# Sorted experts of a two-layer network: gate and up weights become the stationary operand, copied ahead by ScalarE

## The chip, the cores and the metric

The kernel runs on one core of a Trainium2 chip. The metric is the time of one execution on the device, in microseconds, as the median of several executions. TensorE (PE in the rows) does matrix products and transposes, from SBUF into PSUM; VectorE (DVE), ScalarE (ACT) and GpSimd (POOL) do the rest; SyncE's queue (SPq) issues most of the DMAs.

## What is computed

The reference is a network of two layers over 8192 tokens of 128 features. Each layer multiplies an attention branch by a gated expert branch and adds the result to its input. The change lies in the last step, the routed experts of the second layer, where every token goes to one of 32 experts:

```python
topk_ids = jnp.argmax(x @ gate_w, axis=-1)
topk_val = jnp.max(x @ gate_w, axis=-1)
xs = x * jax.nn.sigmoid(topk_val)[:, None]
order = jnp.argsort(topk_ids)
sorted_x = xs[order]
g = _grouped_mm(sorted_x, routed_gate_w, tokens_per_expert)      # 128 -> 256, weights of the row's expert
u = _grouped_mm(sorted_x, routed_up_w, tokens_per_expert)        # 128 -> 256
d = _grouped_mm(jax.nn.silu(g) * u, routed_down_w, tokens_per_expert)  # 256 -> 128
routed_out = d[inv]
...
x = x + s * silu(shared_out + routed_out)
```

Everything is 32-bit float.

## The kernel before

The kernel has four stages, one after the other, with a barrier between them. The first two do the first layer, the third does the second layer's attention branch and the routing. It writes each token as one row of a DRAM tensor `srt`, at a slot that the routing gives it: 96 tiles (`SORTED_TILES`) of 128 rows, each tile with rows of one expert only. A row holds the scaled token (128 values), and behind it a tail of 400 values: a key that names the token, the residual, the attention branch and the shared expert's result. The third stage also leaves a small table `TE` in SBUF that names the expert of each tile; row j of it has eight numbers, those of the four tiles of chunk j-1 and those of the four of chunk j.

The fourth stage, `stage4`, works through the 96 tiles in 24 chunks of four (`IN_FLIGHT`, `n_t`). Chunks 0 and 1 and the last two are written out, those between run in a loop with two chunks in its body, for the two buffers b = 0 and 1. The weights of all 32 experts lie in SBUF (`WE1`, rows call it `big`): per expert 512 columns of gate and up, then 256 of down. For one tile:

- SyncE loads the scaled rows of a chunk (`load`, 256 KB) two chunks ahead, once TensorE has turned the rows that lay in the buffer, and the tails (`load_tail`, 800 KB), once the chunk two before is finished.
- TensorE turns the tile of rows (`row_transpose`, L2041), ScalarE copies it out of PSUM (`rows`, L2100) to `xT`.
- TensorE multiplies (`up`, L2036): the turned rows are the stationary operand, the expert's 512 gate and up columns move past it. The product has tokens in the partitions and hidden features along the row.
- ScalarE applies silu to the gate half (L2110), VectorE multiplies it by the up half (`product`, L2132) into `hb`.
- TensorE turns the product, in two pieces of 128 (`hidden_transpose`, L2046), and VectorE copies it back (`turned`, L2136) to `hT`.
- TensorE multiplies `hT`, stationary, by the down weights in two steps (`down`, L2055) into a quarter of PSUM bank `yp`.

TensorE's order of work is written out by hand. Around tile t it does up(t), the row transpose of t+2, the hidden transpose of t-2 and down(t-3). At the head of a chunk `experts` reads the eight numbers of a row of `TE` into registers (`TENSOR_LOAD`), and these give the addresses of the weights in `WE1`.

Per chunk VectorE adds the shared experts' part (`summed`, L2142), ScalarE takes the silu (`result`, L2104), VectorE multiplies and adds (`weigh` L2147, `finish` L2154 and L2155; the latter increments `done`), and GpSimd scatters the four tiles to the output by four indirect DMAs (`store`, L2191 and L2194). `finish` of chunk 21 stands in chunk 23 behind the product of its third tile, which is tile 94.

## Time and profile before

| | us |
|---|---|
| median of 3 executions | 1386.27 |
| lowest and highest | 1384.61 and 1388.18 |
| the profiled execution's own time | 1387.99 |
| its span, first to last instruction | 1385.5 |
| fourth stage: first row transpose starts | at 1185.99 |
| fourth stage: last store is issued | at 1376.39 |

The profile was taken from one execution, whose own time is 1.7 us above the median; 2.5 us of it lie outside the span. Times in the rows count from the start of the span. An f32 product appears as two records on TensorE, each with a weight load of its own (PEld), so that a product's records come in pairs; a transpose is one record. The idle time of an engine before a row stands in brackets, with what released it.

### The profile page before, as it was taken

Reading aid. Unit: us, or ns where it says so; the run is one execution under the profiler, and the core shown is the slowest. Engines: PE = TensorE matmul, PEld = TensorE weight load, DVE = VectorE, ACT = ScalarE, POOL = GpSimd, SP = SyncE. Lnnn points to the kernel's source line nnn. Section 1 sums busy time; section 2 is a strip of 40 time slices with the busy share of each in tenths; the row PEclk is TensorE's granted clock in tenths of the full one; section 3 lists DMA queues with packets and bytes.
Section 4 is the critical chain, followed back from the end, with each engine's and each line's share of the span. In section 5 each row is a group of like instructions: output and inputs, shape, how many; then the busy total and the mean of one; then the engine's idle time right before and its main releaser. Section 6 shows DMA issues by size and latency. Waiting matters only on the chain. (4 is left out here: it accounts for less than half of the span.)

```text
span 1385.5 us, 28473 instructions
## 1 busy us (share of the span) xinstructions
PE 1191.1 (86%) x7942; PEld 902.7 (65%) x7943; DVE 989.9 (71%) x3562; ACT 783.7 (57%) x1993; POOL 645.9 (47%) x1096
## 2 busy tenths in 40 slices
PE   5999999999972899999999956988888896799993
PEld 3778777777851677767677744766676674456662
DVE  3777777777777777777777636888888886366663
ACT  2575656666630666656565625777777774233331
POOL 3343434343312354545454523556555645056665
PEclk9999999999985999999999977999999999899997
DMA  4424242424301222222222113344344232356651
GB/s 163 144 96 143 88 154 85 150 92 144 127 24 38 51 50 59 44 61 42 61 42 61 35 37 94 113 140 133 120 138 144 91 134 89 119 163 189 184 175 52
DMA packets 140717, 140.83 MB, mean 102 GB/s; under 512 B 18662, under 2 KB 119885, under 8 KB 140672
## 3 DMA queue, kind: packets, MB, share of 16 engines
q1 hardware_dynamic: 125248, 111.38, 25.8%
q0 software_dynamic: 14848, 26.77, 6.9%
q10 hardware_dynamic: 576, 2.15, 0.4%
q8 instruction: 19, 0.31, 0.1%
q14 instruction: 26, 0.21, 0.0%
HBM read 67.63 MB, written 62.13 MB: 94 GB/s over the span
## 5 line engine op out<-in xcount | busy, mean ns | idle before, releaser
L377 ACT ACTIVATE pr<-ps,nmx 128x256 f32<-128x256 f32 x256 | 117.9, 474 | 43.9 <-DVE nmx L424 42.8
L365 ACT ACTIVATE big<-ps,BHS 128x256 f32<-128x256 f32 x256 | 107.1, 470 | 61.3 <-PE ps L242 52.5
L242 PE MATMUL ps<-big,W 128*128 128x256 f32 x512 | 130.9, 400 | 5.6 <-ACT big L370 5.5
L255 PE MATMUL ps<-W,big 128*128 128x128 f32 x1024 | 130.7, 281 | 0.0
L255 PEld LDWEIGHTS ps<-W,big 128*128 128x128 f32 x1024 | 119.6, 192 | 14.0 <-ACT big L365 6.0
L2194 POOL DMA_INDIRECT out<-X,io x96 | 100.5, 1047 | 34.4 <-issue 34.4
L242 PEld LDWEIGHTS ps<-big,W 128*128 128x128 f32 x512 | 95.7, 197 | 26.9 <-ACT big L370 15.7
L2036 PE MATMUL ps<-big,zT 128*128 x192 | 102.5, 616 | 9.6 <-DVE pr L2132 9.1
L424 DVE TENSOR_REDUCE nmx<-ps 128x2 f32<-128x512 f32 x128 | 82.4, 686 | 38.5 <-PE ps L277 21.4
L1003 POOL DMA_INDIRECT ffn<-big,si x64 | 94.0, 1468 | 26.5 <-issue 26.5
L2110 ACT ACTIVATE pr<-ps 128x256 f32<-128x256 f32 x96 | 36.9, 384 | 108.5 <-PE ps L2036 95.4
L432 DVE COPY pT<-ps 128x512 f32<-128x512 f32 x128 | 82.6, 686 | 9.8 <-PE ps L286 9.1
L2132 DVE TENSOR_TENSOR pr<-ps,pr 128x256 f32<-128x256 f32 x96 | 40.7, 424 | 65.7 <-ACT pr L2110 63.3
L510 POOL TENSOR_TENSOR big<-big,EPS 128x2 f32<-128x2 f32 x32 | 6.7, 210 | 155.0 <-DVE big L459 155.0
L277 PE MATMUL ps<-qk 64*128 64x256 f32 x512 | 73.5, 406 | 2.6 <-DVE v L417 2.6
L295 PE MATMUL ps<-pT,v 128*64 128x256 f32 x512 | 69.4, 392 | 3.8 <-DVE pT L432 0.5
L262 PE MATMUL ps<-zT,W 128*128 128x256 f32 x256 | 72.6, 408 | 0.0
L286 PE MATMUL ps<-CST,pr 128*128 128x128 f32 x512 | 68.4, 276 | 1.0 <-ACT pr L377 1.0
L286 PEld LDWEIGHTS ps<-CST,pr 128*128 128x128 f32 x512 | 56.5, 141 | 15.9 <-issue 7.7
L370 ACT ACTIVATE big<-ps,COL 128x256 f32<-128x256 f32 x64 | 36.1, 564 | 53.8 <-PE ps L232 53.8
L415 DVE SCALAR_TENSOR_TENSOR qk<-ps,COL,ROT 128x256 f32<-128x256 f32 x128 | 55.0, 471 | 11.9 <-PE ps L266 9.8
L450 DVE SCALAR_TENSOR_TENSOR big<-ps,rsm,X 128x128 f32<-128x128 f32 x128 | 39.0, 347 | 34.1 <-PE ps L304 25.2
(280 smaller groups left out, 3233.9 us busy)
## 6 DMA issues: line engine op xcount, KB each, us to landing
srt<-big SPq DMA_DIRECT2D x16, 1584.0 KB, 5.7
X<-srt SPq DMA_DIRECT2D x24, 800.0 KB
big<-we SPq DMA_DIRECT2D x16, 768.0 KB, 7.6
big<-we SPq DMA_DIRECT2D x16, 384.0 KB, 3.5
X<-srt SPq DMA_DIRECT2D x24, 256.0 KB
big<-x SPq DMA_DIRECT2D x32, 128.0 KB, 2.2
X<-big SPq DMA_DIRECT2D x32, 128.0 KB, 2.2
xw<-big SPq DMA_DIRECT2D x32, 128.0 KB, 1.9
```

Source lines behind the costliest of these rows:

```text
L242: last = pe.matmul(pb[2 * g + f // 2][:, f % 2 * S:(f % 2 + 1) * S], W0[:, l, 512 + f * P:512 + (f + 1) * P], zT2[:, g, :], start=True, st ...
L255: last = pe.matmul(pb[4 + g][:, t * C:(t + 1) * C], hT[:, g, f, t * P:(t + 1) * P], W0[:, l, 1024 + f * C:1024 + (f + 1) * C], start=(f == ...
L262: pe.matmul(pb[4 + g][:, j * S:(j + 1) * S], w, zT1[:, g, :], start=True, stop=True)
L277: last = pe.matmul(pb[2 * g + h][:, t * S:(t + 1) * S], qk[d, g, 0, t * P:(t + 1) * P], qk[d, g, 1, :], start=True, stop=True)
L286: last = pe.transpose(pb[2 * g + h][:, k * S + t * P:k * S + (t + 1) * P], pr[:, g, h, t, k * P:(k + 1) * P], ident)
L365: act.activation(hT[:, g, f, :], pb[2 * g + half][:, f % 2 * S:(f % 2 + 1) * S], ACT.Silu, bias=BHS[:, l, f:f + 1], scale=GELU).then_inc(s ...
L377: last = act.activation(pr[:, g, h, t, :], pb[2 * g + h][:, t * S:(t + 1) * S], ACT.Exp, bias=nmx[:, g, h * TPU + t:h * TPU + t + 1], accu ...
L424: last = dve.tensor_reduce(nmx[:, g, h * TPU:(h + 1) * TPU], pb[2 * g + h].rearrange("p (t k) -> p t k", t=TPU), X_AXIS, ALU.max, negate=True)
L432: dve.tensor_copy(pT[:, g, h, :, :].rearrange("p k q -> p (k q)"), pb[2 * g + h])\
L1003: pool.indirect_dma_start(out=ffn0[:, :], out_offset=bass.IndirectOffsetOnAxis(ap=si[:, n:n + 1], axis=0), in_=ye[half, n // 2, :], in_off ...
L2036: pe.matmul(gu(k), xT[k % n_t], WE1[:, e, 0:2 * F1], start=True, stop=True).then_inc(s["gu"], 1)
L2194: pool.indirect_dma_start(out=out[:, :], out_offset=bass.IndirectOffsetOnAxis(ap=io[b][:, k:k + 1], axis=0), in_=ob[b][:, k, :], in_offset ...
```

## The change

The gate and up product changes sides. ScalarE copies the 512 gate and up columns of a tile's expert out of `WE1` into one of four fixed buffers `wu` (freed tensors of earlier stages: z, v, att and ROT), four tiles ahead of the silu that stands before the copy. TensorE then uses the four blocks of 128 columns as stationary operands, with the turned rows moving past them, in four products of 128 columns where there was one of 512. The product comes out with hidden features in the partitions, as `down` wants its stationary operand, so that the two hidden transposes of a tile and the copy `turned` are gone. `gu` gets four PSUM banks instead of two. The copy of the turned rows moves from ScalarE to VectorE.

TensorE's order around tile t becomes up(t+2), row transpose of t+4, down(t). The read of a row of `TE` moves on TensorE from the head of a chunk to behind the chunk's first up, and ScalarE reads a row per chunk too. VectorE's `finish` moves from behind the third product of a chunk to behind the first, so that `finish` of chunk 21 stands behind tile 92; `summed` moves from the end of a chunk to behind the second product of the same chunk, `weigh` from the second product to the fourth, of the chunk before. The table `TE` is made by fewer instructions.

```diff
@@ -1842,18 +1842,15 @@
                     def table_rows():
+                        n_c = SORTED_TILES // IN_FLIGHT
+                        dve.memset(TE[:, 0:1, 0:IN_FLIGHT], 0)
+                        dve.memset(TE[:, n_c:n_c + 1, IN_FLIGHT:2 * IN_FLIGHT], 0)
                         dve.wait_ge(s["table"], 1)
...
+                        by_chunk = pb[0][0:1, 0:SORTED_TILES].rearrange("p (j k) -> p j k", k=IN_FLIGHT)
+                        dve.tensor_copy(TE[:, 0:n_c, IN_FLIGHT:2 * IN_FLIGHT], by_chunk)
+                        dve.tensor_copy(TE[:, 1:n_c + 1, 0:IN_FLIGHT], by_chunk)
+                        dve.drain()
+                        dve.tensor_scalar(TE[:, :, :], TE[:, :, :], E1 - 1, None, ALU.bitwise_and)
...
-            s = sems("s4", ["xTp", "xT", "gu", "silu", "h", "hTp", "hT", "yp", "sum", "silu2", "done", "go"])
+            s = sems("s4", ["xTp", "xT", "w", "gu", "silu", "h", "yp", "sum", "silu2", "done", "go"])
...
-            hT = [pT[:, k // 2, k % 2, :, :].rearrange("p a b -> p (a b)")[:, 0:F1] for k in range(n_t)]
+            wu = [b.rearrange("p g t c -> p (g t c)") for b in (z, v, att)] + [ROT[:, :]]
             def gu(k):
-                return ps[:, k % 2, :]
+                return ps[:, k, :]
             def xTp(k):
-                return ps[:, 2 + k % 2, 0:P]
-            def hTp(k):
-                return ps[:, 4 + k % 2, 0:F1]
+                return ps[:, 4 + k % 2, 0:P]
...
-                    def up(t, k, e, first):
+                    def up(t, k):
                         pe.wait_ge(s["xT"], t + 1)
-                        if not first:
-                            pe.wait_ge(s["h"], t - 1)
-                        pe.matmul(gu(k), xT[k % n_t], WE1[:, e, 0:2 * F1], start=True, stop=True).then_inc(s["gu"], 1)
+                        pe.wait_ge(s["w"], t + 1)
+                        if not isinstance(t, int) or t >= n_t:
+                            pe.wait_ge(s["h"], t + 1 - n_t)
+                        for n in range(4):
+                            last = pe.matmul(gu(k)[:, n * P:(n + 1) * P], wu[k][:, n * P:(n + 1) * P], xT[k],
+                                             start=True, stop=True)
+                        last.then_inc(s["gu"], 1)
                     def row_transpose(k, b, pairs):
-                        if k % n_t == 0:
+                        if k == 0:
                             pe.wait_ge(row_in[b], 16 * pairs)
-                        pe.transpose(xTp(k), xt[b][:, k % n_t, :], ident).then_inc(s["xTp"], 1)
-                    def hidden_transpose(t, k):
-                        pe.wait_ge(s["h"], t + 1)
+                        pe.transpose(xTp(k), xt[b][:, k, :], ident).then_inc(s["xTp"], 1)
+                    def down(c, k, b, e):
+                        pe.wait_ge(s["h"], n_t * c + k + 1)
+                        if k == 0 and (not isinstance(c, int) or c >= 2):
+                            pe.wait_ge(s["sum"], c - 1)
                         for f in range(2):
...
-                    def down(t, k, b, e):
-                        pe.wait_ge(s["hT"], t + 1)
-                        if k % n_t == 0 and (not isinstance(t, int) or t >= 2 * n_t):
-                            pe.wait_ge(s["sum"], t // n_t - 1 if isinstance(t, int) else chunk_of[0] - 1)
-                        for f in range(2):
-                            last = pe.matmul(yp(b)[:, k % n_t * C:(k % n_t + 1) * C], hT[k % n_t][:, f * P:(f + 1) * P],
-                                             WE1[:, e, 2 * F1 + f * C:2 * F1 + (f + 1) * C],
+                            last = pe.matmul(yp(b)[:, k * C:(k + 1) * C], hb[k][:, f * P:(f + 1) * P],
+                                             WE1[:, e[k], 2 * F1 + f * C:2 * F1 + (f + 1) * C],
                                              start=(f == 0), stop=(f == 1))
                         last.then_inc(s["yp"], 1)
                     def experts(j):
-                        return nc.values_load_multi_w_load_instructions(
+                        e = nc.values_load_multi_w_load_instructions(
                             TE[0:1, bass.ds(j, 1), :], engines=[mybir.EngineType.PE], min_val=0, max_val=E1 - 1,
                             skip_runtime_bounds_check_because="the table holds a count of experts, clamped to E1 - 1")[1]
-                    chunk_of = [0]
-                    def chunk(q, b, e, first=False, final=False):
-                        chunk_of[0] = 2 * q + b
+                        return e[:n_t], e[n_t:]
+                    def chunk(c, b, q, last=False):
+                        up(n_t * c + 2, 2)
+                        e = experts(c + 1)[0]
                         for k in range(n_t):
-                            t = n_t * (2 * q + b) + k
-                            up(t, k, e[n_t + k], first and k < 2)
-                            if not (final and k >= 2):
-                                row_transpose(k + 2, b if k < 2 else 1 - b, q + 1 + b)
-                            if not (first and k < 2):
-                                hidden_transpose(t - 2, k + 2)
-                            if not (first and k < 3):
-                                down(t - 3, k + 1, b if k == 3 else 1 - b, e[k + 1])
...
+                    for k in range(2):
+                        row_transpose(k, 0, 1)
+                    for k in range(2):
+                        up(k, k)
+                        row_transpose(k + 2, 0, 1)
+                    chunk(0, 0, 0)
+                    chunk(1, 1, 0)
+                    with pe.Fori(1, chunks // 2 - 1) as q:
                         for b in range(2):
+                            chunk(2 * q + b, b, q)
+                    chunk(chunks - 2, 0, chunks // 2 - 1)
+                    chunk(chunks - 1, 1, chunks // 2 - 1, last=True)
                 @block.scalar
                 def _(act):
-                    def rows(t, k):
-                        act.wait_ge(s["xTp"], t + 1)
-                        act.activation(xT[k % n_t], xTp(k), ACT.Copy).then_inc(s["xT"], 1)
+                    def experts(j):
+                        e = nc.values_load_multi_w_load_instructions(
+                            TE[0:1, bass.ds(j, 1), :], engines=[mybir.EngineType.Activation], min_val=0, max_val=E1 - 1,
+                            skip_runtime_bounds_check_because="the table holds a count of experts, clamped to E1 - 1")[1]
+                        return e[:n_t], e[n_t:]
+                    def weights(k, e):
+                        act.activation(wu[k], WE1[:, e[k], 0:2 * F1], ACT.Copy).then_inc(s["w"], 1)
                     def result(j, b):
                         act.wait_ge(s["sum"], j + 1)
                         act.activation(un[b], un[b], ACT.Silu).then_inc(s["silu2"], 1)
-                    def chunk(q, b, first=False, final=False):
+                    def chunk(c, b, last=False):
+                        if not last:
+                            e = experts(c + 1)[1]
                         for k in range(n_t):
-                            t = n_t * (2 * q + b) + k
-                            act.wait_ge(s["gu"], t + 1)
+                            act.wait_ge(s["gu"], n_t * c + k + 1)
                             act.activation(hb[k], gu(k)[:, 0:F1], ACT.Silu).then_inc(s["silu"], 1)
-                            if not (final and k >= 2):
-                                rows(t + 2, k + 2)
-                            if k == 0 and (not isinstance(q, int) or 2 * q + b >= 2):
-                                result(2 * q + b - 2, b)
...
+                    e = experts(0)[1]
+                    for k in range(n_t):
+                        weights(k, e)
+                    chunk(0, 0)
+                    chunk(1, 1)
+                    with act.Fori(1, chunks // 2 - 1) as q:
                         for b in range(2):
+                            chunk(2 * q + b, b)
+                    chunk(chunks - 2, 0)
+                    chunk(chunks - 1, 1, last=True)
+                    result(chunks - 1, 1)
-                    def turned(t, k):
-                        dve.wait_ge(s["hTp"], t + 1)
-                        dve.tensor_copy(hT[k % n_t], hTp(k)).then_inc(s["hT"], 1)
+                    def rows(t, k):
+                        dve.wait_ge(s["xTp"], t + 1)
+                        dve.tensor_copy(xT[k], xTp(k)).then_inc(s["xT"], 1)
...
-                    def chunk(q, b, first=False, second=False):
+                    def chunk(q, b, first=False, second=False, final=False):
                         j = 2 * q + b
                         for k in range(n_t):
-                            t = n_t * j + k
-                            product(t, k)
-                            if not (first and k < 2):
-                                turned(t - 2, k + 2)
-                            if k == 1 and not (first or second):
-                                weigh(b, j - 2)
-                            if k == 2 and not (first or second):
+                            if not (final and k >= 2):
+                                rows(n_t * j + k + 2, (k + 2) % n_t)
+                            product(n_t * j + k, k)
+                            if k == 0 and not (first or second):
                                 finish(q - 1, b, j - 2)
-                        if not first:
-                            summed(q - 1 + b, 1 - b, j - 1)
+                            if k == 1 and not first:
+                                summed(q - 1 + b, 1 - b, j - 1)
+                            if k == 3 and not first:
+                                weigh(1 - b, j - 1)
```

What stands in a row on TensorE at the seam of two chunks inside the loop, before. The first row is the last product of a chunk's last `down`; pT is `hT`, zT is `xT`, pr is `hb`, X the loaded rows and CST the identity.

```order
L2055 MATMUL ps<-big,pT 128x128
L2061 ISA
L2061 TENSOR_LOAD TE
L2033 ISA
L2035 REGISTER_ALU [waits s4_xT]
L2036 ISA [waits s4_h]
L2036 MATMUL ps<-big,zT 128x512
L2041 MATMUL ps<-CST,X 128x128
L2046 MATMUL ps<-CST,pr 128x128 [waits s4_h]
L2046 MATMUL ps<-CST,pr 128x128
L2051 REGISTER_ALU
L2055 ISA [waits s4_hT]
```

The same seam on TensorE now, again from the last product of a `down`; att is one of the four buffers of copied weights.

```order
L2048 MATMUL ps<-big,pr 128x128
L2028 ISA
L2031 REGISTER_ALU [waits s4_w,s4_xT]
L2033 MATMUL ps<-zT,att 128x128 [waits s4_h]
L2033 MATMUL ps<-zT,att 128x128 x3
L2054 ISA
L2054 TENSOR_LOAD TE
L2039 ISA
L2040 MATMUL ps<-CST,X 128x128 [waits s4_row_in0]
L2044 REGISTER_ALU
L2048 ISA [waits s4_sum,s4_h]
L2048 MATMUL ps<-big,pr 128x128
```

The read of the table stood between the last down and the first up; now four products of 128 columns stand ahead of it, and the hidden transposes are gone.

ScalarE at the head of the loop's body before: the silu (pr<-ps), the copy of turned rows (zT<-ps) and `result` (X<-X).

```order
L2110 ACTIVATE pr<-ps 128x256 [waits s4_gu]
L2099 REGISTER_ALU
L2100 ACTIVATE zT<-ps 128x128 [waits s4_xTp]
L2103 REGISTER_ALU
L2104 ACTIVATE X<-X 128x512 [waits s4_sum]
L2109 REGISTER_ALU
L2110 ACTIVATE pr<-ps 128x256 [waits s4_gu]
```

ScalarE at the same place now, with the silu on L2104 and the copies of weights on L2093 (z, v, att and ROT from `big`).

```order
L2087 TENSOR_LOAD TE
L2103 ISA
L2104 ACTIVATE pr<-ps 128x256 [waits s4_gu]
L2093 ISA
L2093 ACTIVATE z<-big 128x512
L2103 REGISTER_ALU
L2104 ACTIVATE pr<-ps 128x256 [waits s4_gu]
L2093 ISA
L2093 ACTIVATE v<-big 128x512
L2103 REGISTER_ALU
```

Each silu has a copy of 512 columns behind it where it had one of 128, and a read of the table stands at the head, where ScalarE had none.

## Rows read from the trace of the kernel before

**Rows 1.** The page: busy time of each engine over the whole span.

```profile
PE 1191.1 (86%) x7942; PEld 902.7 (65%) x7943; DVE 989.9 (71%) x3562; ACT 783.7 (57%) x1993; POOL 645.9 (47%) x1096
```

**Rows 2.** A stretch of the fourth stage: length, engines' busy times, granted clock, DMA, GB/s.

```profile
1300.00:1325.00 25.00, 23.66 (x129) 15.73 (x127) 17.24 (x43) 9.28 (x32) 15.59 (x17) 1.00 0.63 193
```

**Rows 3.** Groups of instructions, 1150 to 1386 us: count, busy, mean ns, idle before.

```profile
L2132 DVE TENSOR_TENSOR pr<-ps,pr 128x256 f32<-128x256 f32 x96 | 40.7, 424 | 65.7 <-ACT pr L2110 63.3 <-issue 1.4
L2110 ACT ACTIVATE pr<-ps 128x256 f32<-128x256 f32 x96 | 36.9, 384 | 108.5 <-PE ps L2036 95.4 <-issue 13.0
L2100 ACT ACTIVATE zT<-ps 128x128 f32<-128x128 f32 x96 | 26.0, 272 | 15.0 <-PE ps L2041 15.0
...
L2104 ACT ACTIVATE X<-X 128x512 f32<-128x512 f32 x24 | 15.2, 632 | 4.8 <-issue 3.4 <-DVE X L2142 1.4
...
L2154 DVE TENSOR_SCALAR io<-X 128x4 int32<-128x4 f32 x24 | 4.1, 171 | 5.5 <-issue 5.0
```

**Rows 4.** Timeline of one tile inside a chunk: start, us, engine, instruction, idle before.

```profile
1256.56 1.02 PE L2036 MATMUL ps<-big,zT 128*128 x2
...
1257.42 0.27 PE L2041 MATMUL ps<-CST,X 128*128 128x128 f32 x1
...
1257.53 0.38 PE L2046 MATMUL ps<-CST,pr 128*128 128x128 f32 x2
1257.62 0.38 ACT L2110 ACTIVATE pr<-ps 128x256 f32<-128x256 f32 x1 [1.08 <-issue]
...
1257.75 0.61 PE L2055 MATMUL ps<-big,pT 128*128 x4
...
1258.04 0.42 DVE L2132 TENSOR_TENSOR pr<-ps,pr 128x256 f32<-128x256 f32 x1 [0.28 <-ACT pr L2110]
...
1258.20 1.02 PE L2036 MATMUL ps<-big,zT 128*128 x2
```

**Rows 5.** Timeline of stage three: four f32 products of 128 columns in a row.

```profile
1134.54 0.97 PEld L1484 LDWEIGHTS ps<-W,pT 128*128 128x128 f32 x8
1134.65 1.06 PE L1484 MATMUL ps<-W,pT 128*128 128x128 f32 x8
...
1135.54 1.89 PE L1430 MATMUL ps<-attT,W 128*128 128x256 f32 x8
```

**Rows 6.** Timeline: first ups of chunks, two in the loop, one written out.

```profile
1260.55 1.12 PE L2036 MATMUL ps<-big,zT 128*128 x2 [0.55 <-DVE pr L2132]
...
1267.62 1.12 PE L2036 MATMUL ps<-big,zT 128*128 x2 [0.28 <-DVE pr L2132]
...
1354.15 1.12 PE L2036 MATMUL ps<-big,zT 128*128 x2
```

**Rows 7.** Timeline: the fourth stage's first tile.

```profile
1182.88 0.94 SPq L2005 DMA_DIRECT2D X<-srt  x2
...
1185.99 0.69 PE L2041 MATMUL ps<-CST,X 128*128 128x128 f32 x2 [12.19 <-DMA X<-srt]
...
1186.95 0.50 PEld L2036 LDWEIGHTS ps<-big,zT 128*128 128x128 f32 x2 [0.67 <-issue]
...
1189.47 0.42 DVE L2132 TENSOR_TENSOR pr<-ps,pr 128x256 f32<-128x256 f32 x1 [13.41 <-ACT pr L2110]
```

**Rows 8.** Timeline: product of tile 94, finish of chunk 21, last sum.

```profile
1358.99 0.42 DVE L2132 TENSOR_TENSOR pr<-ps,pr 128x256 f32<-128x256 f32 x1 [0.28 <-issue]
...
1360.07 0.68 DVE L2155 TENSOR_TENSOR X<-X 128x512 f32<-128x512 f32 x1
...
1365.75 0.69 DVE L2142 TENSOR_TENSOR X<-ps,X 128x512 f32<-128x512 f32 x1 [0.87 <-DMA X<-srt]
```

**Rows 9.** Timeline of GpSimd: the stores of chunks 22 and 23.

```profile
1366.42 0.21 POOL L2191 TENSOR_TENSOR carrier<-carrier 128x1 f32<-128x1 f32 x1
...
1372.16 0.21 POOL L2191 TENSOR_TENSOR carrier<-carrier 128x1 f32<-128x1 f32 x1
...
1376.39 0.97 POOL L2194 DMA_INDIRECT out<-X,io  x1 [0.30 <-issue]
```

More of the change, by code:

```diff
@@ L2075, in chunk @@
-                            if not (first and k < 3):
-                                down(t - 3, k + 1, b if k == 3 else 1 - b, e[k + 1])
-                    def pair(q, first=False, final=False):
-                        for b in range(2):
-                            f, l = first and b == 0, final and b == 1
-                            e = experts(2 * q + b)
-                            chunk(q, b, e, f, l)
-                    for t in range(2):
-                        row_transpose(t, 0, 1)
@@ L2086, in _ @@
-                    pair(0, first=True)
-                    with pe.Fori(1, chunks // 2 - 1) as q:
-                        pair(q)
-                    pair(chunks // 2 - 1, final=True)
-                    t, e = SORTED_TILES, experts(chunks)
-                    for k in range(2):
-                        hidden_transpose(t - 2 + k, 2 + k)
-                        down(t - 3 + k, 1 + k, 1, e[k + 1])
-                    down(t - 1, 3, 1, e[3])
+                            if k and not (last and k > 1):
+                                up(n_t * c + 2 + k, (k + 2) % n_t)
@@ L2104, in result @@
                         act.activation(un[b], un[b], ACT.Silu).then_inc(s["silu2"], 1)
-                    def chunk(q, b, first=False, final=False):
+                    def chunk(c, b, last=False):
+                        if not last:
+                            e = experts(c + 1)[1]
                         for k in range(n_t):
-                            t = n_t * (2 * q + b) + k
-                            act.wait_ge(s["gu"], t + 1)
+                            act.wait_ge(s["gu"], n_t * c + k + 1)
                             act.activation(hb[k], gu(k)[:, 0:F1], ACT.Silu).then_inc(s["silu"], 1)
-                            if not (final and k >= 2):
-                                rows(t + 2, k + 2)
-                            if k == 0 and (not isinstance(q, int) or 2 * q + b >= 2):
-                                result(2 * q + b - 2, b)
-                    def pair(q, first=False, final=False):
-                        for b in range(2):
-                            chunk(q, b, first and b == 0, final and b == 1)
-                    for t in range(2):
-                        rows(t, t)
-                    pair(0, first=True)
-                    with act.Fori(1, chunks // 2 - 1) as q:
-                        pair(q)
-                    pair(chunks // 2 - 1, final=True)
-                    for b in range(2):
-                        result(chunks - 2 + b, b)
+                            if not last:
+                                weights(k, e)
+                            if k == 2 and (not isinstance(c, int) or c):
+                                result(c - 1, 1 - b)
+                    e = experts(0)[1]
+                    for k in range(n_t):
+                        weights(k, e)
+                    chunk(0, 0)
+                    chunk(1, 1)
+                    with act.Fori(1, chunks // 2 - 1) as q:
+                        for b in range(2):
+                            chunk(2 * q + b, b)
+                    chunk(chunks - 2, 0)
+                    chunk(chunks - 1, 1, last=True)
+                    result(chunks - 1, 1)
                 @block.vector
@@ L2173, in pair @@
                             chunk(q, b, first and b == 0, first and b == 1)
+                    for k in range(2):
+                        rows(k, k)
                     pair(0, True)
                     pair(1)
-                    with dve.Fori(2, chunks // 2) as q:
+                    with dve.Fori(2, chunks // 2 - 1) as q:
                         pair(q)
-                    for k in range(2):
-                        turned(SORTED_TILES - 2 + k, 2 + k)
                     last = chunks // 2 - 1
-                    weigh(0, chunks - 2)
+                    chunk(last, 0)
+                    chunk(last, 1, final=True)
                     finish(last, 0, chunks - 2)
```

16 lines of the change are left out of this document (2 added, 14 removed).

## The prediction, made before the changed kernel ran

> **What bounds the kernel now.** I read the page first: TensorE is busy for 86% of the span, more than any other engine [rows 1]. The change touches the fourth stage only (and a few small instructions at the end of the third), so a stretch of that stage comes next: TensorE is busy for 23.66 of 25 us, the clock granted to it is 1.00, its level of 2.4 GHz, and VectorE, ScalarE, GpSimd and the DMA engines are at 69%, 37%, 62% and 63% [rows 2]. The groups say the same from the other side: silu waits before nearly every tile for TensorE's product, 95 us in all, and the copies and products of VectorE wait for silu; only TensorE waits for nearly nothing [rows 3]. TensorE's own order sets the pace.
>
> The timeline of one tile shows how its time is made up [rows 4]. From one start to the next, the up takes 0.86 us, the row transpose 0.11, the two hidden transposes 0.22 and down 0.45: 1.64 us, without a gap. Four such tiles are 6.54 us. At the seam of chunks a gap is added, where the experts' numbers are read: 0.55 us of idle at one seam of the loop, 0.28 at the other, none at a seam that is written out [rows 6]. Over the stage: the product of tile 0 starts at 1189.47 and that of tile 94 at 1358.99 [rows 7, 8], so 169.5 us for 94 tiles, 1.803 us each and 7.21 a chunk. The seam thus costs 0.67 us a chunk beside the tiles.
>
> What ends the kernel is a chain behind this: VectorE's finish of chunk 21 ends at 1360.75 [rows 8], after it GpSimd issues the stores of chunks 21, 22 and 23 without a break and the last begins at 1376.39 [rows 9]; the span ends at 1385.5. That is 24.8 us from the end of this finish, set by GpSimd and the last DMAs, and the change touches none of it.
>
> **The change, part by part.**
>
> *Hidden transposes gone.* 0.22 us a tile on TensorE, which is the engine that paces: 0.88 us a chunk.
>
> *Four products of 128 columns for one of 512.* In stage three four f32 products of 128 columns with a stationary operand each, eight records, take from 1134.65 to the next product's start at 1135.54: 0.89 us, each weight load beside the product ahead of it [rows 5]. One of 512 takes 0.86. So +0.03 us a tile. The Trainium skill (TensorE: Matmul & The Clock Gate, Back-to-back issue gap) speaks against the change here: it gives about 81 ns for a product of 128 columns in a stream of loads and products, against an isolated gap of about 56, so that weight loads would not all hide; by it the up would take 0.89 x 81/56 = 1.29 us, 0.4 us a tile more. Rows 5 show 111 ns for a record of an f32 product together with its load, so the trace does not bear it out, and I take 0.89.
>
> A tile is then 0.89 + 0.11 + 0.45 = 1.45 us on TensorE, a chunk 5.80.
>
> *The seam.* The read of the table now stands behind an up, with 0.89 us of products queued ahead of it. How long a read takes no row shows by itself. The nearest is the stage's start: the transposes start at 1185.99 and the first up's weight load, behind the read, at 1186.95 [rows 7], so the read with what goes with it took at most 0.96 us, if it began no earlier than the transposes. That is about what the products ahead of it cover. What stays is the arithmetic on registers for the loop's waits: the seams inside the loop have 0.3 to 0.5 us more idle than the one written out [rows 6]. Lower bound for the seam: 0. Upper: the 0.67 of now. I take 0.35, about the extra of the loop. A chunk: 6.15 us, between 5.80 and 6.47.
>
> *ScalarE.* It loses the copy of rows (0.272) and gains a copy of 512 columns. Its nearest row is the silu of 512 columns in SBUF, 0.632 [rows 3]. Per chunk: 4 x (0.384 + 0.632) + 0.632 for `result` = 4.70 us, and the table's read. Behind the last copy of a chunk, which covers 0.63 of it, 0.33 of the 0.96 would show: 5.03. If nothing is covered, 5.66. Both are under 6.15. These copies run four tiles ahead of their ups, and at the start of the stage there are 4.1 us between SyncE's first load at 1182.88 and the first up at 1186.95, in which ScalarE has nothing else to do [rows 7]: room for the read and the first copies, 0.96 + 2 x 0.63 = 2.2 us. I cost them at nothing; without that cover each would be 0.63 on TensorE.
>
> *Silu and product must come back in time.* Now down(t) stands two tiles behind up(t), so h is wanted at 2 x 1.45 + 1.0 = 3.9 us after the start of up(t). Silu starts 1.06 us after the up and the product of VectorE ends 1.90 after it (1256.56 to 1258.46) [rows 4]. There are 2.0 us of slack. What can delay silu is one copy and `result`, 0.63 each, and the read; they do not add up to 2.0.
>
> *VectorE.* It loses `turned` (128x256) and gains the copy of rows (128x128, about the 0.27 that ScalarE takes). Per chunk 4 x (0.27 + 0.424) + 3 x 0.69 + 0.17 = 5.0 us [rows 3, 8], under 6.15. It is next in line, not the bound.
>
> *GpSimd.* From one store's start to the next without a wait is 1372.16 - 1366.42 = 5.74 us [rows 9]. Under 6.15, but close: a floor under all gains.
>
> *Loads of the tails.* A tail was 5.0 us in coming at the end (finish done 1360.75, first use 1365.75, idle for the DMA before it) [rows 8]. Now `finish` stands behind the first product, and `summed` of the next chunk's second slot wants the tail five tiles later less the 0.95 us of finish itself: 5 x 1.54 - 0.95 = 6.7 us. Covered; if the load of rows that is issued just ahead (256 KB against 800) stretches it by a third, 6.6, and it is just covered. DMA traffic rises by 7.21/6.15, from 193 to 226 GB/s, and the DMA engines' share from 0.63 to 0.74 [rows 2].
>
> *Table.* Made in the shadow of the last scatters of stage three, whose landing the barrier awaits. Nothing.
>
> **The sum.** Tile 0's product comes when it did (one transpose, copy, up and silu ahead of it). `finish` of chunk 21 stands behind tile 92 in place of 94. So 92 x 6.15/4 = 141.5 us in place of 169.5: 28.0 us less, of which 3.1 come from the two tiles and 24.9 from 23.5 chunks at 1.06. From there the end follows 24.8 us later as before. The profiled execution's 1387.99 becomes 1360.0; against the median of 1386.27, 1.7 us lower, it is 1358.3. I predict 1358. With 5.80 us a chunk it is 1350, with 6.47 1366.
>
> **Rivals.**
>
> *A. ScalarE paces.* If the read holds ScalarE for its whole length, nothing overlaps, and each copy's address costs another 0.1 to 0.2 us, a chunk is 5.66 + 4 x 0.2 + a hand-over for each of nine instructions of about 0.04, 6.8 us: 156.4 in place of 169.5, 1373. Against it: ScalarE is idle for half the stage now and its queue has only these ten things to do. The Trainium skill (Runtime: NRT & Kernel Launch, Instruction fetch mechanics) gives about 200 ns for each register loaded; a row of the table has eight, so 1.6 us by this page. ScalarE would then be at 4.70 + 1.6 = 6.3 us a chunk, and TensorE at 5.80 + 1.6 - 0.89 = 6.5, which gives about 1366 by this page. The 0.96 of rows 7 speaks against so long a read, unless it ran during the wait for the DMA. Chance of A and of anything else that puts a chunk at 6.5 to 7.1 (tails that land late among them): 0.18.
>
> *B. No change.* Something else paces at 7.2, as GpSimd would if its stores were slower under more DMA traffic: from 5.74 it would need another 1.4 us a chunk. In the loop it idles before each chunk's first store now. 1386 less the 3 us at the end. Chance 0.03.
>
> *C. Slower: weight loads don't hide.* An up has eight loads, each before a record of 0.11 us; if a load takes as long as the record and none hides, a tile is 1.45 + 8 x 0.11 = 2.33 us, and the kernel is 92 x 2.33 - 169.5 = 45 us slower, 1431. It decides from the point where a chunk takes 7.4 us, 0.39 us exposed per tile, less than half of this. Rows 5 speak against it, with the same shapes and type; what they don't have is a wait ahead of each group. Chance 0.05.
>
> The forecast, 5.80 to 6.5 us a chunk, has 0.74. The range: 1350 is the bound with no seam at all; upward it reaches into A, to 1371, which leaves out most of B and C and the end of A, under 2 in 10. Faster by over 0.3% (4 us, about what a measurement can tell here) 0.92, same 0.03, slower 0.05.
>
> **What the profile will show.** The groups: 768 records of ups (8 a tile) instead of 192, no 128x128 products of `hb` with the identity, 96 ScalarE copies of 128x512 at about 0.63. Start to start of ups about 1.45 inside a chunk and 1.8 at the seam. Silu's idle time before it much smaller, ScalarE at about 80% and VectorE at 85% of the stage. GpSimd with almost no wait before its stores. Granted clock still 1.00. The prediction is wrong if a tile inside a chunk takes more than 1.5 us on TensorE, if TensorE waits for `w`, `h` or `xT` in steady state, or if the seam keeps 0.67 us or more.

## The result, and the profile after

The changed kernel took 1380.85 us (median of 20 runs, 1370.43 to 1390.45), the kernel before 1387.18 us beside it (20 runs, 1384.61 to 1389.41): a ratio of 0.9957, interval 0.9942 to 0.9972. The forecast was 1358, range 1350 to 1371. The gain is 6.3 us where 28 were forecast, and the runs spread over 20 us where those of before spread over 5. "The first measurement" below means these runs.

The window that answers [rows 2] (length, then busy time and instructions of PE, PEld, DVE, ACT and POOL, granted clock, DMA share, GB/s):

```profile
core 0 of [0], span 1374.7 us
...
1300.00:1325.00 25.00, 23.52 (x195) 22.21 (x195) 16.27 (x44) 14.61 (x34) 16.65 (x19) 1.00 0.62 202
```

TensorE is at 94%, where it was at 95% before, but it no longer sets the pace. Its timeline over one chunk (start of the eight products of each up):

```profile
1258.76 1.16 PE L2033 MATMUL ps<-zT,ROT 128*128 128x128 f32 x8 [0.31 <-DVE zT L2130]
...
1260.31 1.06 PE L2033 MATMUL ps<-zT,z 128*128 128x128 f32 x8
...
1261.76 1.06 PE L2033 MATMUL ps<-zT,v 128*128 128x128 f32 x8
...
1264.21 1.15 PE L2033 MATMUL ps<-zT,att 128*128 128x128 f32 x8 [0.84 <-issue]
...
1265.96 1.06 PE L2033 MATMUL ps<-zT,ROT 128*128 128x128 f32 x8
...
1267.41 1.06 PE L2033 MATMUL ps<-zT,z 128*128 128x128 f32 x8
```

Where nothing interferes a tile is 1.45 us, as forecast (1260.31 to 1261.76, 1265.96 to 1267.41). But from one z to the next, a chunk, it is 7.10 us: one tile took 2.45 and one 1.75. The waits of the stage show for whom each engine waited (1200 to 1345 us: us in all, times, longest; "remote" is a releaser that the profile could not name):

```profile
ACT pr L2104 <- PE ps L2033: 47.8, 33, 2.4
...
DVE zT L2130 <- PE ps L2040: 30.8, 28, 2.4
...
ACT pr L2104 <- remote: 12.8, 9, 3.1
...
PE ps L2033 <- DVE zT L2130: 6.9, 11, 2.0
DVE zT L2130 <- remote: 5.7, 2, 3.1
```

The last line but one is what the forecast said would prove it wrong: TensorE waits for `xT`, up to 2.0 us. VectorE's copy into `xT` in turn waits for a row transpose that was done long before. The tile of 2.45 us comes about so:

```profile
1261.20 0.27 PE L2040 MATMUL ps<-CST,X 128*128 128x128 f32 x1
...
1263.78 0.29 DVE L2130 COPY zT<-ps 128x128 f32<-128x128 f32 x1 [1.87 <-PE ps L2040]
```

The transpose for the tile that uses att ends at 1261.47. The copy of it starts at 1263.78, with VectorE idle for 1.87 us before it, and the up of att, due at 1263.21, starts at 1264.21. All engines' timeline at a second such place:

```profile
1267.41 1.06 PE L2033 MATMUL ps<-zT,z 128*128 128x128 f32 x8
...
1268.31 0.27 PE L2040 MATMUL ps<-CST,X 128*128 128x128 f32 x1
...
1269.79 0.39 ACT L2104 ACTIVATE pr<-ps 128x256 f32<-128x256 f32 x1 [1.79 <-PE ps L2033]
1269.82 0.29 DVE L2130 COPY zT<-ps 128x128 f32<-128x128 f32 x1 [1.29 <-PE ps L2040]
```

The up ends at 1268.47, the transpose at 1268.58; silu and copy, which wait for two different instructions, both start at 1269.8, within 0.03 us. Both engines were free. What was late is the news. The trace also records the updates of semaphores, by which one engine tells another that it is done: those of this up and this transpose stand at 1269.76 and 1269.80, 1.29 and 1.22 us after the ends, and that of the transpose of 1261.20 at 1263.76, 2.29 us after.

The record of updates has gaps: none stands between 1267.60 and 1269.76. Such gaps of over 0.8 us, in the 135 us from 1195 on, are 18, together 27.8 us; in the trace of before there is one, of 1.5 us. They are not stretches in which no semaphore was updated, because the record is incomplete: of some 14360 updates of this kernel (e9 below) this trace has 12297. In the gap from 1249.92 to 1251.24 stand these two rows:

```profile
1249.82 0.38 ACT L2104 ACTIVATE pr<-ps 128x256 f32<-128x256 f32 x1 [2.21 <-PE ps L2033]
...
1250.23 0.42 DVE L2126 TENSOR_TENSOR pr<-ps,pr 128x256 f32<-128x256 f32 x1
```

VectorE's product waits for this silu and starts 0.03 us after its end, so that ScalarE's update came at once and was only not recorded. Sorted by engine, the updates that are on record say whose are late. Of 226 by TensorE (for ups, transposes and downs) 90 stand over 0.3 us after the instruction's end, up to 2.2; of 225 by VectorE and ScalarE (copies, products, silus) not one does, the latest being 12 ns. (Each is measured from the last end before it of an instruction of its kind, which makes a late one look less late.) TensorE's ends are worked out by the profile; where nothing is late, all 278 of e9 stand within 15 ns of them. The late ones were held and not made late: in this trace the updates of two successive ups often stand 0.19 us apart, less than the 0.89 us that the products of one up take. The forecast has no term for this.

### The profile page after: what moved, and what is told of

Same layout as the page of the kernel before. It is cut to its first block and busy times, and to the rows that moved or that the text cites. A ratio compares the mean times of both kernels' runs of the same rounds, so it can differ in the third digit from the quotient of the medians.

```text
span 1374.7 us, 29258 instructions
## 1 busy us (share of the span) xinstructions
PE 1187.2 (86%) x8326; PEld 948.2 (69%) x8327; DVE 978.5 (71%) x3556; ACT 813.4 (59%) x1994; POOL 640.4 (47%) x1096
## 5 line engine op out<-in xcount | busy, mean ns | idle before, releaser
L2188 POOL DMA_INDIRECT out<-X,io x96 | 97.0, 1010 | 34.4 <-issue 34.4
L2104 ACT ACTIVATE pr<-ps 128x256 f32<-128x256 f32 x96 | 36.6, 381 | 69.6 <-PE ps L2033 56.6
L2130 DVE COPY zT<-ps 128x128 f32<-128x128 f32 x96 | 27.5, 287 | 58.0 <-PE ps L2040 49.4
L1350 POOL TENSOR_TENSOR W<-W,EPS 128x2 f32<-128x2 f32 (+1 forms) x48 | 10.2, 212 | 112.5 <-DVE W L1735 59.6
```

The costliest lines, as they stand in the source:

```text
L2188: pool.indirect_dma_start(out=out[:, :], out_offset=bass.IndirectOffsetOnAxis(ap=io[b][:, k:k + 1], axis=0), in_=ob[b][:, k, :], in_offset ...
```

## The experiments

Each job runs on one chip of the machine, whose number the result gives; the kernel before is timed in every job. The first job (chip 11) started from what stands in the timeline beside the gaps, which I took for pauses of all semaphores: SyncE now issues the rows' and the tail's load mostly 0.6 to 0.8 us apart, and ScalarE's new read of the table follows. "Stalls" below are the waits for late updates.

**Loads apart** (e1): the tail first, the rows two tiles later.

```
 if not first: wait(done, j - 1); load_tail(j, b)
-if not last:  wait(xTp, n_t*j + n_t)   (ahead of the tail)
+if not last:  wait(silu, n_t*j + 4); load(j + 2, b)
```

> The changed kernel, but SyncE issues a chunk's tail load (800 KB) first and the next load of rows (256 KB) only when silu of the fourth tile of the chunk is done, about 3 us later, in place of 0.7 us before the tail. Theory 1 (the two loads issued together hold back TensorE's and the other engines' semaphore updates for 1 to 3 us, while the data moves): the seams fall to the shortest ones seen, 6.2 to 6.3 us a chunk, the stage loses 15 to 20 us and the kernel comes to 1355 to 1365 with little spread. Rival 2 (ScalarE's copies of 512 columns are what delays) and rival 3 (ScalarE's read of the table is): no change, 1376 to 1385.

**The kernel before with both loads together** (e2): `load` also waits for `done`, right ahead of `load_tail`.

> The kernel before, but the load of rows is held until the chunk two before is finished, so that it is issued right ahead of the tail load, as in the changed kernel; no other edit. Theory 1: late semaphore updates appear in the kernel before too, silu and the copies start 1 to 2 us late once a chunk, and it becomes slower by 10 to 25 us, with a larger spread. Rivals 2 and 3: no late updates, time within 3 us of 1387.

**Short copies** (e3), `act.activation(wu[k][:, 0:8], WE1[:, e[k], 0:8], ACT.Copy)`: the rest of the weights is stale, so other products.

> The changed kernel with ScalarE's copies of the weights cut from 512 columns to 8; the products then use stale weights, so the output is not the reference's. Theory 1: the holes in the semaphore updates stay, 1372 to 1383. Rival 2: they go, 1355 to 1362. Rival 3: as theory 1.

**No read by ScalarE** (e4): `e = experts(c + 1)[1]` is left out of its chunks, so other experts.

> The changed kernel with ScalarE reading the table once, for the first chunk, and copying the weights of these four experts for all chunks; the gate and up products then use the wrong experts, so the output is not the reference's. Theory 1 and rival 2: the holes stay, 1376 to 1383. Rival 3 (the reads of the table by ScalarE hold the semaphore updates): they go, 1355 to 1362.

Measured against 1386.27 of before: 1351.3 (ratio 0.9757, 0.9743 to 0.977), 1386.69 (1.0001, 0.9991 to 1.0011), 1350.61 (0.9741, 0.9726 to 0.9756) and 1352.15 (0.9757, 0.9742 to 0.9772). Any one of three edits seemed to cure the stalls, and bringing the loads together in the kernel before (e2) had done no harm. I took this for an interplay, with the read's place in the stream of the loads as theory A.

The second job (chip 6) moved the read and the loads. **e5 and e6** put it behind the weights of the first and of the third tile of a chunk; the numbers then come from the next row of the table, half for this chunk, half for the next:

```
-e = experts(c + 1)[1]; for k in range(n_t): silu(c, k); weights(k, e)
+o, n = experts(c + 2)
+for k in range(p, n_t): silu(c, k);     weights(k, o)      (p = 1 or 3)
+for k in range(p):      silu(c + 1, k); weights(k, n)
```

> The changed kernel, with ScalarE's read of the expert numbers moved behind the weights of a chunk's first tile (its products are the same); loads as changed. In the runs without stalls that place is some 1.5 us before the tail load is issued, in place of 2.4 us behind it (0.8 to 1.9 us behind it once stalls have shifted it). Theory A (a read of ScalarE that falls just behind the issue of row and tail load holds back every engine's semaphores until the tail has moved): no stalls, 1349 to 1355 us. Theory B (any read of ScalarE in a chunk whose two loads stand together does it, wherever it is): about 1380 us again. Theory C (the two loads together are to blame in a chunk this short, the read only adds): between, 1365 to 1385 us.

> The same with the read behind the third tile's weights and the result's silu: some 1.0 to 1.6 us behind the tail's issue in a chunk that runs without a stall, so right where the stalls of the changed kernel begin. Theory A: stalls in most chunks, 1380 us or more. Theory B: about 1380 us. Theory C: as the run with the read after the first tile.

**e7**: in VectorE's `chunk`, `if k == 1` in place of `if k == 0` ahead of `finish`.

> The changed kernel with VectorE's last step of a chunk (and so the tail load, which waits for it) one tile of 1.45 us later; ScalarE's read stays where it is. Row and tail load are then some 2 us apart, and the read comes about 1 us behind the tail's issue. Theory A in its narrow form (what counts is the read's distance from the tail's issue): stalls, 1375 to 1395 us. If what counts is that the two loads stand back to back: 1349 to 1356 us.

**e8**: e2 with `experts(2 * q + b)` in ScalarE's chunk.

> The kernel before, with its row load held back until the tail load's place (which alone left the time at 1386.7 us), and in addition a read of a row of the table by ScalarE in each chunk, whose numbers nothing uses, about 1.5 us behind the tail's issue. Theory A: stalls of 1 to 2 us in many chunks and 10 to 35 us more, 1396 to 1420 us. If it takes ScalarE's long copies or the shorter chunk as well: 1386 to 1389 us.

1350.89 (0.975, 0.9733 to 0.9766), 1351.74 (0.9753, 0.9736 to 0.977), 1351.88 (0.9767, 0.974 to 0.9794) and 1385.59 (1.0002, 0.9992 to 1.0011; its read isn't in the trace, since nothing used its numbers, so it repeats e2). In e6 the read started mostly 0.8 to 2.2 us behind the tail's issue, where theory A had to stall, and there is no gap in its trace. All three theories seemed to fall. What no run had told yet was whether the changed kernel itself stalled on this chip; if not, none of these runs tests a theory of the stalls.

> The changed kernel itself, unaltered. Seven kernels one edit away from it (loads apart, short copies, no read, read in two other places, last step later) have all come out near 1351 us, which none of theories A to C explains. If the stalls belong to the changed kernel's own phases: 1370 to 1390 us again, with pauses of 1 to 2 us in most chunks. If they belonged to the chip or the moment at which it was measured and not to the kernel: 1349 to 1355 us, and then nothing in the kernel needs explaining.

**e10**: e8, with the numbers used by four copies of 8 columns.

> The kernel before with both loads together and a read of the table by ScalarE in each chunk, whose numbers now address four copies of 8 columns (a read that nothing used had been dropped from the program). Theory A: 1396 to 1420 us. If a read beside the loads costs nothing outside the changed kernel's own arrangement: 1386 to 1390 us.

Chip 6 again: the unaltered kernel took **1351.19 us** (1349.86 to 1354.42; ratio 0.9749, 0.9732 to 0.9765), e10 1385.57 (1.0002, 0.9993 to 1.0012). So the six edits of it before (its expectation counts seven) had cured nothing on this chip: there was nothing to cure. For chip 11, where the unaltered kernel never ran, the same is inferred. Window, waits (1200 to 1345 us) and TensorE's timeline of the changed kernel on chip 6:

```profile
core 0 of [0], span 1352.5 us
...
1300.00:1325.00 25.00, 25.00 (x227) 25.00 (x226) 19.58 (x53) 18.29 (x41) 19.29 (x22) 1.00 0.64 205
```

```profile
ACT pr L2104 <- PE ps L2033: 37.6, 68, 1.1
POOL out L2188 <- issue: 31.6, 96, 0.6
POOL carrier L2185 <- DVE X L2149: 19.5, 3, 18.8
...
DVE X L2136 <- DMA X<-srt: 3.8, 5, 1.3
```

```profile
1261.04 1.06 PE L2033 MATMUL ps<-zT,z 128*128 128x128 f32 x8
1261.93 0.27 PE L2040 MATMUL ps<-CST,X 128*128 128x128 f32 x1
...
1262.49 1.06 PE L2033 MATMUL ps<-zT,v 128*128 128x128 f32 x8
...
1263.94 1.06 PE L2033 MATMUL ps<-zT,att 128*128 128x128 f32 x8
...
1265.39 1.06 PE L2033 MATMUL ps<-zT,ROT 128*128 128x128 f32 x8
...
1266.84 1.06 PE L2033 MATMUL ps<-zT,z 128*128 128x128 f32 x8
```

TensorE is busy for 25.00 of 25 us and waits for nobody; every step is 1.45 us, the one over the read (v to att) too, and a chunk is 5.80. Silu waits often and briefly, for products that are being made, at most 1.1 us.

The third job asked whether the level goes with the job, and tried to provoke the stalls.

> The changed kernel unaltered once more, in a job of its own. It measured 1380.85 us (20 runs, none below 1370) at first and 1351.2 us in the last job. If the stalls go with the job or the chip and not with the kernel, each job gives one level or the other for all its runs: all within 1349 to 1356 us, or all within 1370 to 1391 us, and hardly a mix inside one job.

**e12**: `e = experts(c + 1)[0]` ahead of `up(n_t * c + 2, 2)`.

> The changed kernel with TensorE's read of the table put ahead of the third tile's up product, with nothing queued behind which the read could pass. This is the seam that the forecast priced at 0 to 0.67 us a chunk for the changed kernel. If the seam is really hidden by the product now, this kernel pays it back: 24 chunks by 0.3 to 0.67 us, 7 to 16 us more than the changed kernel in the same job (1358 to 1367 us where that has 1351). If the read costs TensorE nothing in either place: no more than 2 us apart.

**e13**: behind `load_tail`, `sp.dma_start(spare, srt_t[:, bass.ds(n_t * j, 2), C:ROWW])`.

> The changed kernel with a further load of 410 KB a chunk behind the tail load, into a tile that nothing uses. If the stalls of the first measurement are DMA pressure that the changed kernel's shorter chunk reaches now and then: pauses of 1 us and more in most chunks, 1365 to 1400 us. If pressure of this size is harmless to the semaphores: 1350 to 1358 us (a rows load that lands a little later, nothing else).

> The kernel of the first experiment (tail load first, row load two tiles later) again, beside the changed kernel in one job. If the changed kernel stalls in this job and this one does not, the distance of the loads matters on such a chip after all; if both are near 1351 us, the distance is worth less than 1 us.

It fell on chip 12, and the stalls were there: 1385.58 (1376.54 to 1392.08, 12 runs; ratio 0.998, 0.9957 to 1.0002), 1380.24 (0.9954, 0.9939 to 0.9969), 1387.96 (1.0002, 0.9984 to 1.002) and 1382.4 (0.9962, 0.9946 to 0.9977). The kernel before took 1386.99, its usual time (but for one run of 6488.53 among 32, unexplained). Not one of the 39 runs of the four came below 1376. Window and waits of the changed kernel, chip 12:

```profile
core 0 of [0], span 1383.4 us
...
1300.00:1325.00 25.00, 21.63 (x176) 20.09 (x176) 14.83 (x40) 13.07 (x29) 13.84 (x18) 1.00 0.55 177
```

```profile
ACT pr L2104 <- PE ps L2033: 40.5, 30, 2.4
DVE zT L2130 <- PE ps L2040: 25.4, 25, 2.4
ACT pr L2104 <- remote: 22.2, 9, 3.5
DVE zT L2130 <- remote: 14.1, 6, 3.0
PE ps L2033 <- DVE zT L2130: 12.9, 13, 2.6
```

176 of TensorE's records in these 25 us, where chip 6 has 227, and the same signature as in the first trace: fewer and longer waits, up to 3.5 us. Loads apart, with the very kernel of e1, was no cure here: its window of the same 25 us reads

```profile
1300.00:1325.00 25.00, 20.81 (x157) 19.54 (x157) 13.58 (x37) 12.70 (x29) 13.46 (x17) 0.93 0.57 179
```

where TensorE was busy for 20.81 of 25 us and its granted clock is 0.93 in place of 1.00. More traffic didn't clearly add to the stalls (1387.96 against 1385.58, within the spread of both).

The last two jobs were to show which part makes the kernel sensitive, and fell on chips 1 and 4.

> The changed kernel without ScalarE's read of the table in the chunks (its copies take the first row's experts throughout, so the products are other ones), once more, since its first run fell into a job in which the changed kernel itself was not timed. In a job on the chip of the third run of the changed kernel (chip 12, where it and three neighbours of it stalled): if ScalarE's read starts the stalls, 1349 to 1356 us; if not, 1370 to 1392 us. On another chip: 1349 to 1354 us, which tells nothing of the stalls.

> The changed kernel with ScalarE copying 8 columns of each tile's weights in place of 512 (other products) once more. On chip 12: if ScalarE's long copies are needed for the stalls, 1349 to 1356 us; if not, 1370 to 1392 us. On another chip: 1349 to 1354 us.

> TensorE's read of the table ahead of the third tile's up product once more, since its first run fell on chip 12, where stalls drown it. On a chip without the stalls the changed kernel takes 1351.2 us. If the seam that the forecast priced (0 to 0.67 us a chunk) is hidden by the product in the changed kernel and comes back here: 1358 to 1367 us. If TensorE's read costs it nothing in either place: within 2 us of 1351 us. On chip 12: 1377 to 1388 us, which tells nothing.

> The changed kernel without ScalarE's reads of the table in the chunks (other products) a third time. On chip 12: 1349 to 1356 us if ScalarE's read starts the stalls, 1370 to 1392 us if it does not. On another chip 1349 to 1354 us, which tells nothing of the stalls.

1351.41 (0.9751, 0.9734 to 0.9768), 1350.99 (0.9749, 0.9733 to 0.9766), 1349.4 (0.9749, 0.9732 to 0.9765) and 1349.6 (0.9755, 0.9738 to 0.9771): nothing on the stalls, but e17 settles the seam. Its ratio is that of the changed kernel on chip 6, and TensorE's timeline has the read ahead of att:

```profile
1262.07 1.06 PE L2033 MATMUL ps<-zT,z 128*128 128x128 f32 x8
...
1263.52 1.06 PE L2033 MATMUL ps<-zT,v 128*128 128x128 f32 x8
...
1264.97 1.06 PE L2033 MATMUL ps<-zT,att 128*128 128x128 f32 x8
```

1.45 us again. The read costs TensorE nothing that shows, in front of the product or behind it.

Worked out from the traces' records of semaphores and reads: gaps over 0.8 us between 1195 and 1330 us; those that begin 0.4 to 1.1 us after a read of ScalarE has begun; all updates on record in the whole trace; and TensorE's updates of ups, transposes and downs between 1195 and 1330 us, with those over 0.3 us late.

```
kernel                    chip  gaps  sum, us  after a read  on record  TensorE's  late
before                       -     1      1.5             -      12552        275    29
loads together (e2)         11     0      0               -      14543        300     0
before, read used (e10)      6     0      0               -      14535        300     0
changed, first time          -    18     27.8            11      12297        226    90
changed (e9)                 6     0      0               -      14356        278     0
changed (e11)               12    24     31.2            12      12337        208    91
read ahead (e12)            12    27     34.5            13      12348        209    90
more traffic (e13)          12    18     24.4             9      12724        205    84
loads apart (e14)           12    24     28.9            10      12292        215    93
loads apart (e1)            11     1      0.8             0      14402        273     0
read after tile 3 (e6)       6     0      0               -      14385        273     0
```

Of VectorE's and ScalarE's updates for copies, products and silus not one is late in any of these traces. Two things appear that the gaps alone hide. Late updates and missing records go together. And the trace of the kernel before has them too: 29 late, up to 1.17 us, and a record shorter by a seventh than that of the nearly same kernel e2. ScalarE reads no table in that kernel.

## Why the prediction was wrong, point by point

**Hidden transposes, four products for one: right.** A tile is 1.45 us on TensorE in the rows of every measurement shown, where nothing is late. The weight loads hide (eight records in 1.06 us, the next instruction's beginning before their end); rival C is out. The 1.29 us that I worked out for the up from the 81 ns of the Trainium skill (TensorE: Matmul & The Clock Gate, Back-to-back issue gap) is not borne out: it is 0.89. The scaling by 81/56 was mine; eight records at 81 ns would be an estimate of 0.65 us by that page, which the rows don't bear out either.

**The seam: mis-sized.** I took 0.35 us a chunk from the idle at the seams of before [rows 6] and from a read of at most 0.96 us. It is 0: 5.80 us a chunk in e9 and e17. In the sum this is 92 x 0.35/4 = 8 us: 1358 becomes 1350, and the changed kernel took 1351.2 on chip 6 and e17, with only the read moved, 1349.4 on chip 4. The read itself, in the traces' records, takes TensorE 0.59 us. The moving of the read, a part of the change, bought nothing (e12's order is as fast, e17). That the idle of [rows 6] was no cost of the read either is argued, not tried: its releaser is VectorE's product, a wait that the two tiles between up and down have ended.

**ScalarE: right.** Its copies are 0.62 us (0.632 forecast), its read 0.55, and 18.29 of 25 us are 4.24 a chunk (4.70 forecast; each copy starts about 0.1 us before the silu ahead of it ends). The kernel is no faster with copies of 8 columns (e3, e16), nor with no read at all (e4, e15, e18): ScalarE doesn't pace, rival A is out. The Trainium skill's about 200 ns a register (Runtime: NRT & Kernel Launch, Instruction fetch mechanics), 1.6 us for eight, is not borne out by these reads of a row in SBUF: 0.54 to 0.76 us.

**Tails: nearly right.** Not quite covered: in e9 `summed` waited for a tail five times, at most 1.3 us. TensorE waited for none.

**GpSimd: right, and nearer than thought.** Only 3 waits for `finish` are left in the stretch from 1200 to 1345 us, where the chunk takes 5.80 and its floor was put at 5.74 [rows 9]. Where nothing is late, TensorE's chunk is now 0.06 us above GpSimd's floor; that a faster TensorE would gain no more than this is argued, not tried.

**Silu and product must come back in time: the step that failed.** Its 2.0 us of slack counted what the engines have to do (0.63, 0.63 and the read). It took for granted that an engine which waits hears at once, and put late news at nothing. In the first measurement, as on chip 12, TensorE's updates came up to 2.3 and 3.0 us late. Nor was silu's path the short one. TensorE's waits name `xT` (11 in the first trace, up to 2.0 us), and the way from the row transpose by VectorE's copy to the up has less slack, which the forecast left out. In e9 the transpose of 1261.93 ends at 1262.20 and its up starts at 1263.94; less 0.29 for the copy and 0.03 for the hand-over, 1.4 us are left. An update 2.29 us late leaves a delay of 0.9 us, and the tile took 1.0 us too long.

The size agrees. From tile 0's product to tile 92's, the stretch that the forecast put at 141.5 us, e9 took 132.9 us, the first trace 157.9 and e11 169.5; from there to the end of the span all three took about 26. So the whole excess lies where the updates are late. No rival had this in it.

What is shown: the level goes with the chip or the job and not with one run (20 runs, and 39, without one below 1370); and in the jobs where the changed kernel and its neighbours lost 30 us, the kernel before took 1387, only 0.7 to 2.6 us more than in the other jobs. Late updates reach it too, 29 in the trace of before, but up to 1.17 us only, and it bears them. That the first measurement ran on a chip like 12 is inferred, from the same late updates, spread and level.

What stays open is why the updates come late and what in the change makes them more and later. Half of the gaps begin 0.4 to 1.1 us after ScalarE has begun a read, where an even spread over 7.1 us would put a tenth. But late updates occur without any read by ScalarE, in the kernel before; in the changed ones a read also follows the tail's issue by mostly 0.8 to 3 us; and neither the kernel without the read nor the one with short copies ever ran on such a chip. A rival that no run tests is the recording itself: it loses updates in the traces that have late ones, and no run here was timed without a record.

## What to carry to other kernels

Time the changed kernel itself, unaltered, in every job in which its neighbours are timed: six edits that each "cured" the stalls meant nothing until the ninth run showed that there was none to cure on that chip. When two engines that wait for different instructions start within a few hundredths of a microsecond of each other, long after both were done, compare the updates of semaphores with the instructions' ends, engine by engine. First count whether the record is complete: a gap in it is not a pause if an engine that waits starts within it. And work out the slack of every path back to the engine that paces, the short ones too. And where an instruction has products queued ahead of it, as the read of the table has, its price is what is left over of them, here nothing in either order.

## What the runs showed of the hardware that was not expected

On some chips, or at some times, TensorE's updates of semaphores reach the waiting engines up to 3 us late, once 4.7 (e14), several times in 7 us of this loop, and successive ones then follow 0.19 us apart in place of 1.45; those of VectorE and ScalarE that are on record come within 13 ns. One kernel so has two levels, 1351 and 1380 to 1386 us, each for a whole job, while another keeps its time within 0.2% across such jobs. Where updates are late, a seventh of them is missing from the record. A read of eight registers took ScalarE 0.55 and TensorE 0.59 us. A stream of f32 products of 128 columns with their loads ran at 111 ns a record, eight in 0.89 us, at the full clock of 2.4 GHz.
